# An S4 convolution and a ternary FFN on one core: head tiles regrouped, four convolutions moved ahead of the loop, and the loop's engine orders rewritten

## What is computed

```
K[h, l]   = 2 Re sum_n Cs[h, n] exp(dtA[h, n] l)          # 32 heads, 64 modes, 512 steps
u         = x masked to s < length[b]
c         = (causal convolution of u[b, h] with K[h] + u D[h]) masked again
xq        = clip(round(c sqrt7 / (mean|c| + eps)), -8, 7)  # and its scale beta, per row
gate, up  = xq @ ternary(w_gate).T, xq @ ternary(w_up).T   # 512 -> 1376
inter     = up * relu(gate)^2, rounded to int8 with the row's maximum
out       = x + inter @ ternary(w_down).T                  # 1376 -> 512
```

## Time and profile before

| | us |
|---|---|
| median of 3 runs | 231.75 |
| lowest and highest of them | 231.63, 232.09 |
| span of the profiled execution | 230.7 |
| PE busy (share of the span) | 189.2 (82%) |
| VectorE busy | 170.3 (74%) |
| ScalarE busy | 116.9 (51%) |
| GpSimd busy | 6.3 (3%) |

### The profile page before, as it was taken

The page is one execution under the profiler, slowest core; times in us unless marked ns, Lnnn a source line. Parts: engine busy times, 40 slices in busy tenths (PEclk is TensorE's granted clock), DMA queues, the critical chain, the costliest instruction groups (busy, mean ns, idle before and its releaser), DMA issues.

```text
span 230.7 us, 3519 instructions
## 1 busy us (share of the span) xinstructions
PE 189.2 (82%) x1187; PEld 97.6 (42%) x1187; DVE 170.3 (74%) x473; ACT 116.9 (51%) x185; POOL 6.3 (3%) x21
## 2 busy tenths in 40 slices
PE   1001288995795999999999999999999999998882
PEld 1001256643354444454544444454544444444340
DVE  6999639379668567869696967869696967869681
ACT  0256754495677081836546281836546281735510
POOL 7030000000000000000000000000000000000000
PEclk9999997999799999999999999999999999999999
DMA  3799307926654562846567594846657594442613
GB/s 73 281 280 378 67 1 184 399 95 162 165 132 118 107 183 45 236 97 205 121 171 160 135 224 113 234 94 205 127 165 163 138 230 102 108 94 59 129 36 82
DMA packets 38610, 35.18 MB, mean 153 GB/s; under 512 B 24513, under 2 KB 24577, under 8 KB 38593
## 3 DMA queue, kind: packets, MB, share of 16 engines
q1 hardware_dynamic: 38304, 34.96, 57.1%
q0 software_dynamic: 160, 0.00, 0.0%
q10 hardware_dynamic: 128, 0.00, 0.0%
HBM read 25.27 MB, written 4.28 MB: 128 GB/s over the span
## 4 chain that ended last, share of the span: by engine, by line
PE 58%; DVE 5%; ACT 4%; issue 4%; DMA 2%; DVEq 0%; ACTq 0%
PE down_ps L595 16%; PE gate_ps L556 13%; PE up_ps L558 12%; PE conv_ps L451 12%; PE tr_act_ps L441 2%; DMA it_int<-inter_q 2%; ACT int_down L645 1%; DVE inter L1051 1%; DVE imax L1055 1%; PE tr_dve_ps L464 1%; ACT g L710 1%; ACT g L713 1%; DVE down_t L972 1%; PE conv_ps L511 1%; DVE inter_q L1104 0%
## 5 line engine op out<-in xcount | busy, mean ns | idle before, releaser
L556 PE MATMUL gate_ps<-gate_t,q_t 128*128 128x416 bf16 (+2 forms) x192 | 69.3, 361 | 2.1 <-DVE q_t L991 1.1
L558 PE MATMUL up_ps<-up_t,q_t 128*128 128x416 bf16 (+2 forms) x192 | 69.3, 361 | 0.0
L710 ACT ACTIVATE g<-gate_ps,gu_scale 128x416 f32<-128x416 f32 (+2 forms) x48 | 30.3, 631 | 73.1 <-issue 57.9
L1051 DVE SCALAR_TENSOR_TENSOR inter<-up_ps,gu_scale,g 128x416 f32<-128x416 f32 (+2 forms) x48 | 33.3, 693 | 31.1 <-ACT g L713 31.0
L595 PE MATMUL down_ps<-down_t,i_t 128*128 128x512 bf16 (+1 forms) x176 | 40.8, 380 | 2.2 <-DVE down_t L972 1.3
L451 PE MATMUL conv_ps<-toep,x_t 128*64 128x512 f32 (+3 forms) x256 | 38.0, 439 | 1.4 <-ACT x_t L662 1.4
L1055 DVE TENSOR_REDUCE imax<-inter 128x1 f32<-128x416 f32 (+2 forms) x48 | 30.3, 631 | 1.7
L713 ACT ACTIVATE g<-g 128x416 f32<-128x416 f32 (+2 forms) x48 | 28.1, 585 | 1.5
L556 PEld LDWEIGHTS gate_ps<-gate_t,q_t 128*128 128x128 bf16 x192 | 18.8, 98 | 23.6 <-issue 7.3
L595 PEld LDWEIGHTS down_ps<-down_t,i_t 128*128 128x128 bf16 (+1 forms) x176 | 15.9, 98 | 24.7 <-DVE i_t L1072 5.5
L451 PEld LDWEIGHTS conv_ps<-toep,x_t 128*64 128x64 f32 x256 | 17.0, 136 | 21.0 <-issue 15.7
(11 more groups left out here) (173 smaller groups left out, 178.3 us busy)
## 6 DMA issues: line engine op xcount, KB each, us to landing
toep<-k_back SPq DMA_DIRECT2D x16, 512.0 KB, 5.2
x_in<-in_x_dram SPq DMA_DIRECT2D x32, 128.0 KB, 2.8
x_res<-in_x_dram SPq DMA_DIRECT2D x32, 128.0 KB, 4.0
out_dram<-o_sb SPq DMA_DIRECT2D x32, 128.0 KB, 2.5
raw_gate<-in_L_ffn_w_gate_dram SPq DMA_DIRECT2D x1, 1536.0 KB, 9.9
raw_up<-in_L_ffn_w_up_dram SPq DMA_DIRECT2D x1, 1536.0 KB, 15.8
raw_down<-in_L_ffn_w_down_dram SPq DMA_DIRECT2D x1, 1536.0 KB, 9.7
raw_down<-in_L_ffn_w_down_dram SPq DMA_DIRECT2D x1, 1216.0 KB, 12.3
```

The source lines that it names most:

```text
L556: pe.matmul(gate_ps[bank][:, 0:cn], q_t[p][:, i, :], gate_t[:, i, c0:c0 + cn], start=(i == 0), stop=(i == KB - 1))
L558: mm = pe.matmul(up_ps[bank][:, 0:cn], q_t[p][:, i, :], up_t[:, i, c0:c0 + cn], start=(i == 0), stop=(i == KB - 1))
L710: nc.scalar.activation(g2[bank][:, 0:cn], gate_ps[bank][:, 0:cn], ACT.Relu, scale=gu_scale[p][:, 0:1]).then_inc(relu_done, 1)
L1051: v.scalar_tensor_tensor(out=inter[:, c0:c0 + cn], in0=up_ps[bank][:, 0:cn], scalar=gu_scale[p][:, 1:2], in1=g2[bank][:, 0:cn], op0=ALU.mu ...
```

## The change

The kernel is rewritten in most of its parts. What it computes stays the same.

- **Tiles.** Tile t now holds the heads t and 16 + t (before: 2t and 2t + 1). So the first four heads of each half of K are what the first four tiles need.
- **K tables.** VectorE raises powers (`raise_powers`, `left_factors`) for the first EARLY = 4 head pairs only; GpSimd does the other 12 pairs, with 28 two-input instructions of up to 384 elements per partition. `k_sums(1)` on PE, which waits for them, stands in iteration 0 after the second chunk.
- **Convolutions.** `conv(0)` to `conv(3)` stand before the loop, and iteration m does `xt(m + 4)` and `conv(m + 4)`, so that iterations 12 to 15 have none. There are 4 Toeplitz buffers, 2 for the transposed x, 4 for y.
- **x** is loaded once, four tiles in one load (`load_quad`), partly into the storage of the weights that are done with, and kept for the residual.
- **The rounded tile** is transposed by a DMA (`turn_q`) two tiles ahead; only tile 0 goes through PE (`first_q`). PE's `qt` is gone from the loop.
- **Chunks.** The four gate matmuls come first, then the four up ones, with a semaphore each, and relu waits for the gate ones alone.
- **w_down** shares storage with `w_gate`. Both halves of its sum are on ScalarE, in iteration 0; its transposes are nine groups in a row in iteration 1, all after the third chunk.
- **i_t** is double buffered, and its cast stands after the second `gated` instead of before it.
- Weight rows are laid out so that a partition's rows are contiguous in DRAM. Of 19 keep-clock products 12 remain.

The diff, cut to its core:

```diff
+    EARLY = 4
...
+        def raise_powers(tt, settle, cols, k, n, u, v):
+            w = pw[:, 0, cols, 0].shape[1]
...
+            tt(us, re, by, ALU.mult)
+            settle(tt(vs, im, by, ALU.mult))
+            tt(pw[:, 0, cols, k + 1:k + n + 1], us[:, 0], vs[:, 1], ALU.subtract)
+            settle(tt(pw[:, 1, cols, k + 1:k + n + 1], us[:, 1], vs[:, 0], ALU.add))
...
         def _(sp):
...
+            load_toep(0)
+            load_toep(1)
+            load_toep(2)
+            for i in range(2):
+                sp.wait_ge(w_rounded[0][i], 1)
             down_rows = w_down.rearrange("(c p) i -> p c i", p=P)
             for i in range(2):
                 s = weight_part(2, i)
                 sp.dma_start(raw[2][s], down_rows[s]).then_inc(w_loaded[2][i], 16)
+            load_toep(3)
...
+            load_quad(1)
...
+            turn_q(1)
             store_k(1)
...
+            sp.wait_ge(k_stored[1], 32)
+            load_toep(4)
...
+                if m == 0:
+                    load_quad(2)
...
+                if m + 2 < T:
+                    turn_q(m + 2)
+                if m + 5 < T:
+                    load_toep(m + 5)
...
         def _(pe):
...
+            def mean(m):
+                pe.wait_ge(w_summed, 2 * m + 2)
+                if m == 2:
+                    pe.wait_ge(xt_copied, EARLY + 1)
...
+            for m in range(T):
+                products(m, 0)
+                products(m, 1)
+                if m == 0:
+                    pe.wait_ge(rest_tables, 1)
+                    k_sums(1)
+                if m + EARLY < T:
+                    xt(m + EARLY)
+                products(m, 2)
+                if m == 0:
+                    mean(2)
+                if m == 1:
+                    for g in range(len(DOWN)):
+                        turn_down(g)
+                if m >= 1:
+                    down(m - 1)
+                if m + EARLY < T:
+                    conv(m + EARLY)
...
         def _(act):
...
+                relu_square(0)
+                if m == 0:
+                    weight_sum(2, 0)
+                if m + 2 < T:
+                    y_sum(m + 2)
+                relu_square(1)
+                if m == 0:
+                    weight_sum(2, 1)
+                if m + 2 < T:
+                    y_round(m + 2)
+                relu_square(2)
+                if m + EARLY < T:
+                    xt_copy(m + EARLY)
...
         def _(dve):
...
-                if 1 <= k < T:
-                    dve.wait_ge(it_loaded, 16 * m)
-                    wait(dve, down_done, m - 1)
-                    v.tensor_copy(i_t[:], it_int[:]).then_inc(it_dve_copied, 1)
...
+                wait(dve, inter_quant, m)
+                gated(0)
+                if m + 2 < T:
+                    y_scale(m + 2)
+                gated(1)
+                if m == 0:
+                    k_copy(1)
+                    weight_mean(2)
...
+                if m >= 1:
+                    dve.wait_ge(it_loaded[(m - 1) % 2], 16 * ((m - 1) // 2 + 1))
+                    wait(dve, down_done, m - 2)
+                    v.tensor_copy(i_t[(m - 1) % 2][:], it_int[(m - 1) % 2][:]).then_inc(it_copied, 1)
+                step(gated(2))
...
+                if m == 1:
+                    for g in DOWN_DVE:
+                        down_copy(g)
```

879 lines of the change are left out of this document (417 added, 462 removed).

## The result

The changed kernel is slower. Its median is 243.4 us (240.24 to 244.13) against 231.92 us (231.63 to 233.22) for the kernel before on the same chip, a ratio of 1.045 with a 95% interval of 1.038 to 1.053. Medians here are over all executions, while ratios and intervals leave out the slow ones, over 1.5% above the fastest of their kernel (among them one of four here, six of twelve in e1_cast and two of four in e8_all), so a ratio is not the quotient of two medians. The forecast was 238.3 us with a range of 230.5 to 243.5. The sign and the mechanisms in the loop held, the one of the loop's start did not, and the size was 5.1 us short. The median lies 0.1 us inside the range, while the four executions spread over 3.9 us: that it fell inside is luck.

What follows compares the result with a forecast made beforehand. PE's list was taken as the bound in iterations 2 to 13. Terms -2.6 + 5.4 + 5.1 + 3.2 - 4.5 = +6.6 gave a span of 237.3 and a time of 238.3 us, range 230.5 to 243.5.

Steps and rivals of the forecast that it cites:

- term A: Start of the loop: first product at 47.0 instead of 49.65 us, -2.6 us, bounds -4.5 to -1.
- D: Iterations 2 to 11: down waits for the later cast, period 10.69 instead of 10.37 us, +3.2 us in all.
- B: Iteration 0: late convolution, started cold, 19.5 instead of 14.10 us, +5.4 us, bounds +3 to +7.
- Both paths: Iteration 0: ScalarE's chain with w_down's sums to 11.8 us; K copy, stores and Toeplitz load to the convolution at 15.1 us.
- C: Iteration 1: turned groups wait for VectorE's copies behind inter_q, down starts cold; 20.9 instead of 15.82 us, +5.1 us.
- E: Iterations 12 to 14: no convolution left; 12 and 13 take 8.38 us each, 14 takes 8.2, together -4.5 us.
- At nothing: Items priced at zero: x loads, DMA transposes of q, and GpSimd's tables, ready at 40 us with 10 us to spare.
- rival of late tables: GpSimd's tables come after 50 us and hold PE ahead of iteration 0's third chunk; 242.8 us, chance 0.12.
- a cast that doesn't bind: In the loop down doesn't wait for VectorE's cast, D falls by 6.4 us; 231.9 us, chance 0.08.
- the faster one: PE's gaps in prologue and iterations 0 and 1 absorb the moved convolutions, B and C add nothing; 227.8 us, chance 0.14.
- the clock stays up: In iterations 0 and 1 the clock stays up or falls once for little; 233.1 us, chance 0.2.

Runs made afterwards that it cites:

- e1_cast: Changed kernel with the cast of i_t ahead of the second gated product again; 234.78 us, 0.997 of the kernel before.
- e8_all: Changed kernel with e2_toep3, e4_k_early, e5_sums and e6_turns together, cast ahead of the second gated product in iterations 1 to 12; 218.83 us, 0.934 of before.
- e2_toep3: Changed kernel with the load of Toeplitz tile 3 issued behind tiles 0 to 2, ahead of w_down's loads; 238.21 us, 1.020 of before.
- e10_prologue: On e9: three turned groups of w_gate ahead of the x tiles, ScalarE's and VectorE's prologue steps reordered, four fillers dropped; 220.83 us against 221.01.
- e4_k_early: Changed kernel with k_sums(1) ahead of convolution 3 and k_copy(1) behind y_mask(2), both before the loop; 239.68 us, 1.027 of before.
- e5_sums: On e4_k_early: both sums of w_down before the loop, mean(2) behind iteration 0's second products; 232.62 us, 0.998 of before.
- e7_clock_full: Changed kernel with 19, 11 and 15 unused filler products in PE's gaps of iterations 0 and 1; 244.26 us.
- e6_turns: Changed kernel with turn_down groups 0 to 3 between iteration 1's products, copies spread between VectorE's and ScalarE's steps; 241.18 us, 1.041 of before.
- e9: On e8_all: turned groups and their copies earlier, ScalarE's x copy earlier, 1 MB x load behind the transpose of q; 221.01 us, 0.948 of before.
- e11: On e7_clock_full: only the 1 MB load of x tiles 8 to 11 moved behind the transpose of q(2) and Toeplitz tile 5; 243.7 us against 244.26.
- e12: On e9: 1 MB load of x tiles 8 to 11 moved to iteration 2, turned groups later; 221.95 us, 0.953 of before.

## Why the prediction was right, and where it was short

**The 5.1 us.** 3.65 of them are term A and 0.4 are D; 0.75 lie outside the span (1.8 us where I had 1.05, the median of the runs less the profiled span), and 0.3 are the profiled execution against the median.

**A failed, by 3.65 us.** The step was "From there PE's list was 22.25 us; it loses the 2.3 us of idle": I took PE's list from the first weight transpose to the first product as free of waits. The start of that list was 0.9 us later than my 27.5 (28.37, behind x at 25.61), and one wait of 3.00 us stands in it. I had followed the loads of x and `w_up` through SyncE's queue, but not that of Toeplitz tile 3, which the change puts behind `w_down`. With that one load moved (e2_toep3) the first product is at 46.81 us, against the forecast's 47.0. PE's wait for x is not what set the first product: in e10_prologue, with that wait covered, the sum over `w_up` and Toeplitz tile 0 came next.

**B was right in sum, 19.33 for 19.5.** `mean(2)` started 11.27 us into the iteration (forecast 11.8 for the copy ahead of it), the convolution at 14.86 (15.1), and it lost 2.15 us to the lower level (2.1). Both paths are shown: the K path by e4_k_early (2.73 us shorter) and ScalarE's sums by e5_sums (7.6 more). What I hadn't seen is that the 2.1 us of the clock can't be had by themselves: e7_clock_full took them out of the convolution, and iteration 1 gave them back.

**C was right in size, 21.06 for 20.9, and half right in cause.** The waits for VectorE's copies behind `inter_q` and the slow `down` are there (1.41 us over 2.55, where I had 2.1), and e6_turns removes 5.05 us. But VectorE was late for a further reason, 3.6 us for `q_int` of tile 2. I had written that the DMA transposes of q "have more than an iteration of time". That is so in the steady loop, not where the load of four x tiles stands ahead of one. It cost next to nothing in this kernel: `inter_q` started 8.22 us into the iteration, against 7.89 in a steady one, and the first copy 9.08 (forecast 9.0).

**D and E were right.** `down` waits for `i_t` in each iteration, 11.2 us over the loop by the page. The price of the late cast is more than the 0.64 us of the forecast, though. Without it the period is 9.87, not 10.05, so it costs 0.86: the changed list was shorter than I had it. Between the second and the third chunk the four transposes of x take 0.44 us to the next product (105.72 to 106.16 us in e1_cast), where they had taken 0.61 (196.77 to 197.38 us before), and I had counted only the 0.32 us of `qt`.

**At nothing:** GpSimd's tables, taken as ready at 40 us, were ready at 38.6 (38.00 + 0.59). That is partly luck: the 28 instructions took 17.4 us from 21.2 us on, in the lower part of the 6 to 36 us that I had, and 384 elements took 0.93 us, where the slope of the two small products would have given 2.8. The rival of late tables and the one of a cast that doesn't bind have fallen; so has the faster one, since iterations 0 and 1 took 40.39 us together. The rival "the clock stays up" didn't come true (0.75 and 0.82 in the two iterations); that its 5.2 us would have been gained isn't shown either, as e7_clock_full kept the clock up in iteration 0 only and was not faster.

**The scatter.** Four runs of the changed kernel spread over 3.9 us, and 7 to 13 of the kernel before, in the later sets, over 2.9 to 4.2. The lower clock behind the wait ahead of convolution 3 can account for some 2 us of it (convolution 3 took 2.38 to 4.54 us in six traces); what else moves it stays open.

## What to carry to other kernels

When a change rebuilds the order of loads, follow every load through the issuing queue and compare each landing with its first reader, also that of a small load behind a big one: 0.5 MB behind 2.75 MB landed after 16.2 us, and moving one line was worth 4 to 5 us. A cast that an engine's list puts one step later can cost the whole gain of a rebuilt loop, since it is paid in each iteration; look for it where the slack of its reader is zero. And a stage with waits on several engines gives back what is taken out of one wait, so measure the stages together, and the whole.

## What I had not expected of the hardware

- A DMA transpose of 128 x 512 or 128 x 1408 two-byte elements landed in 2.4 and 3.5 us at best. In thirteen cases, in eleven traces, one was issued 1.2 to 2.5 us after a 1 MB load of x in the same queue, and landed after 6.0 to 10.1 us (8.7 in the changed kernel, 8.9 in e7, 7.2 and 6.0 in e8, 10.1 in e9, 8.4 in e11, 8.3 in e12). In eleven cases it was issued 2.7 to 3.6 us after, and landed after 4.2 to 6.6 us, and once after 9.4, with two such loads on the way (e12).
- The granted clock isn't all: in the changed kernel's prologue the row for 25.60 to 31.00 us gives 1.00, though the transposes and fillers there had the pace of the lower level. Eight transposes took 0.85 us there, 0.45 us later on, and a filler 0.43 us against 0.22.

```profile
25.60:31.00 5.40, 4.62 (x33) 4.19 (x34) 0.68 (x1) 3.68 (x5) 5.08 (x10) 1.00 0.22 46
```

```profile
30.93 1.91 PE L548 MATMUL conv_ps<-steps,ident_bf 128*128 128x512 bf16 x4
```
